# Reciprocal roots of a cross-attention block: one GpSimd power operation in place of eight VectorE steps

## The reference, cut to what matters

```
def _layernorm(x):  m = mean(x); v = var(x); return (x - m) / sqrt(v + 1e-5)
def _rmsnorm(t):    return t * rsqrt(mean(t * t, axis=-1) + 1e-6)        # over the 8 features of a head
q = rmsnorm(heads(layernorm(x) @ Wq.T));  k, v = heads(ctx @ Wk.T, ctx @ Wv.T);  k = rmsnorm(k)
x = x + tanh(g_xattn) * softmax(q k^T / sqrt(8)) v
y = layernorm(x)
x = x + tanh(g_ffn) * down(silu(gate(y)) * up(y))                        # down, gate, up: (w - 128) * scale
```

## Time and profile before

| | |
|---|---|
| Three timed runs | 256.37, 257.71, 260.33 us (median 257.71) |
| Profiled execution, first to last instruction (its own time is recorded as this span alone) | 254.6 us |
| PE busy | 217.0 us, 85% |
| DVE busy | 189.1 us, 74% |
| ACT busy | 176.9 us, 69% |
| POOL busy | 107.6 us, 42% |
| Mean granted clock of PE | 0.966 of full speed |
| Chain that ended last: PE, DVE, issue, ACT | 62%, 17%, 8%, 7% |
| One pass of the loop (two tiles) | 25.05 us |

### The profile page before, as it was taken

One profiled execution on the slowest core, in us unless ns is written; L12 is line 12 of the kernel. 1 busy time (PEld: TensorE's weight loads), 2 busy tenths in 40 slices (PEclk: granted clock), 3 DMA queues, 4 the chain that ended last, 5 costly groups with the idle time before them and its releaser, 6 DMA issues.

```text
span 254.6 us, 7326 instructions
## 1 busy us (share of the span) xinstructions
PE 217.0 (85%) x2592; PEld 175.6 (69%) x2592; DVE 189.1 (74%) x583; ACT 176.9 (69%) x338; POOL 107.6 (42%) x145
## 2 busy tenths in 40 slices
PE   1664878949869999999999999999999998983974
PEld 1553746727558888778878887888788776773873
DVE  4587999872878778786878687968796887667163
ACT  3358593746877896879688958895889588455261
POOL 5012303031314382737184728463835473454442
PEclk9999996777999999999999999999999999999799
DMA  6798631405061524141323223322315041000001
GB/s 176 220 351 209 72 58 21 86 5 107 0 106 35 71 23 86 36 108 33 70 47 97 42 61 61 83 56 51 76 50 64 21 82 48 21 24 0 21 21 41
DMA packets 45128, 18.08 MB, mean 71 GB/s; under 512 B 36401, under 2 KB 44849, under 8 KB 45105
## 3 DMA queue, kind: packets, MB, share of 16 engines
q1 hardware_dynamic: 45104, 17.77, 32.9%
HBM read 7.28 MB, written 2.10 MB: 37 GB/s over the span
## 4 chain that ended last, share of the span: by engine, by line
PE 62%; DVE 17%; issue 8%; ACT 7%; DMA 2%; POOL 2%; SPq 1%; DVEq 0%; ACTq 0%
PE bank L1371 16%; PE bank L1286 14%; PE pv_ps L1250 10%; PE bank L1396 9%; PE score_ps L1231 5%; DVE silu L983 2%; PE bank L1319 2%; ACT probs L530 2%; DVE hidden L998 2%; ACT tanh_g L645 2%; DMA w_raw<-L_xattn_Wv_dram 2%; DVE xc_lo L894 1%; PE bank L1277 1%; PE bank L1273 1%; PE bank L1351 1%
## 5 line engine op out<-in xcount | busy, mean ns | idle before, releaser
L530 ACT ACTIVATE probs<-score_ps 128x1024 f32<-128x1024 f32 x64 | 66.0, 1033 | 2.7 <-PE score_ps L1231 2.7
L466 POOL TENSOR_TENSOR qk_unit<-qk_raw,root_y 128x512 f32<-128x512 f32 x16 | 17.4, 1084 | 86.0 <-DVE root_y L788 86.0
L1371 PE MATMUL bank<-x_hi,gu_hi 128*128 128x256 f32 (+1 forms) x192 | 49.8, 296 | 4.0 <-DVE hidden L998 2.0
L1250 PE MATMUL pv_ps<-probs,v_blocks 128*32 128x128 f32 x1024 | 43.0, 287 | 6.3 <-issue 3.8
L1371 PE MATMUL bank<-x_lo,gu_hi 128*128 128x256 f32 (+1 forms) x192 | 47.1, 281 | 0.0
L434 POOL TENSOR_TENSOR h_lo<-hidden,h_hi 128x256 fp32r<-128x256 f32 (+1 forms) x48 | 36.7, 772 | 21.1 <-ACT h_hi L656 20.3
L1371 PEld LDWEIGHTS bank<-x_hi,gu_hi 128*128 128x128 f32 (+1 forms) x192 | 34.3, 179 | 8.8 <-issue 4.6
L1250 PEld LDWEIGHTS pv_ps<-probs,v_blocks 128*32 128x32 f32 x1024 | 25.1, 112 | 15.8 <-issue 6.6
L1286 PE MATMUL bank<-w_hi,xc_hi 128*128 128x256 f32 x96 | 31.7, 330 | 3.8 <-DVE xc_lo L894 3.8
L1371 PEld LDWEIGHTS bank<-x_lo,gu_hi 128*128 128x128 f32 (+1 forms) x192 | 34.5, 180 | 0.0
L645 ACT ACTIVATE tanh_g<-bank,half_gate 128x256 f32<-128x256 f32 (+1 forms) x48 | 22.7, 474 | 14.8 <-PE bank L1371 13.4
(11 more groups left out here) (108 smaller groups left out, 438.0 us busy)
## 6 DMA issues: line engine op xcount, KB each, us to landing
ctx_sb<-ctx_dram SPq DMA_DIRECT2D x16, 128.0 KB, 2.6
out_dram<-x_all SPq DMA_DIRECT2D x16, 128.0 KB, 1.8
x_all<-x_dram SPq DMA_DIRECT2D x1, 1536.0 KB, 11.3
dn_int<-L_ffn_wq_down_dram SPq DMA_DIRECT2D x1, 704.0 KB, 7.6
gu_int<-L_ffn_wq_gate_dram SPq DMA_DIRECT2D x1, 640.0 KB, 4.6
gu_int<-L_ffn_wq_up_dram SPq DMA_DIRECT2D x1, 640.0 KB, 5.6
x_all<-x_dram SPq DMA_DIRECT2D x1, 384.0 KB, 4.5
w_raw<-L_xattn_Wq_dram SPq DMA_DIRECT2D x1, 256.0 KB, 2.7
```

Source lines behind the costliest of these rows:

```text
L530: nc.scalar.activation(probs[:, t % 2, :], score_ps[t % 2][:].rearrange("p h n -> p (h n)"), ACT.Exp, scale=float(HD) ** 0.5 / UNIT ** 2). ...
L1250: last = nc.tensor.matmul(pv_ps[BLOCK * quadrant:BLOCK * (quadrant + 1), region * P:(region + 1) * P], v_blocks[:, e, h * BLOCK:(h + 1) * ...
L1371: last = nc.tensor.matmul(bank[k][0:r, a * TOK:(a + 1) * TOK], w[:, j, a, c, 0:r], xx[:, c, :], start=(n == 1), stop=(n == (4 if wide_weig ...
```

## The change

The bit estimate and `root_chain` go. POOL does `root_y = root_in ** minus_half` as one `tensor_tensor` with the operation `pow` and a tensor filled with -0.5, for each tile, and likewise for the three batches of x. `roots` moves from DVE's list to POOL's, in front of `qk_norm`; DVE, which now waits for `root_ready` where it waited for the last step, goes on in the meantime with what stands between. `x_roots(0)` stands on POOL ahead of the filling of `v_blocks`. `x_offsets(1)` moves on DVE from behind the means of its batch to behind `root_inputs(-1, 0)`, and `x_offsets(2)` to behind `root_inputs(0, 0)`. The buffers of the middle steps go.

```diff
+            nc.gpsimd.memset(minus_half[:], -0.5).then_inc(half_ready, 1)
+            pool.wait_ge(half_ready, 1)
+            def x_roots(i):
+                first, last = BATCHES[i]
+                pool.wait_ge(x_eps_added, i + 1)
+                nc.gpsimd.tensor_tensor(x_root[:, first:last], x_var[:, first:last], minus_half[:, 0:last - first],
+                                        ALU.pow).then_inc(x_root_ready, 1)
+            x_roots(0)
             nc.gpsimd.memset(v_blocks[:], 0.0).then_inc(v_zeroed, 1)
...
+            x_roots(1)
+            def roots(p, e):
+                b = 2 * p + e
+                if not has_roots(p, b):
+                    return
+                if has_tile(p, b + 2):
+                    pool.wait_ge(eps_added, b + 3)
+                    if since(b, -1):
+                        pool.wait_ge(qk_hi_ready, b + 2)
+                        pool.wait_ge(unit_ready, b + 2)
+                if has_tile(p, b - 1):
+                    pool.wait_ge(root_in_ready, b)
+                if since(b, 2):
+                    pool.wait_ge(x1_bias_ready, b - 1)
+                    pool.wait_ge(x1n_ready, b - 1)
+                nc.gpsimd.tensor_tensor(root_y[:], root_in[:], minus_half[:], ALU.pow).then_inc(root_ready, 1)
...
             def iteration(p):                                   # POOL
+                if isinstance(p, int) and p == FIRST + 1:
+                    x_roots(2)
                 add_attention(p, 0)
                 split_chunks(p - 1, 1, (0, 1))
+                roots(p, 0)
                 qk_norm(p, 0)
                 split_chunks(p, 2, (2,))
                 split_qk(p, 0)
                 split_chunks(p, 2, (3, 4, 5))
                 add_attention(p, 1)
+                roots(p, 1)
                 qk_norm(p, 1)
                 split_qk(p, 1)
...
-            def root_chain(buffers, cols, count, before, first=1, last=ROOT_STEPS):
-                ...                                             # seven scalar_tensor_tensor
...
-                nc.vector.tensor_scalar(root_y[:].bitcast(I32), root_in[:].bitcast(I32), -0.5, START_BITS, ALU.mult,
-                                        ALU.add).then_inc(root_steps, 1)
...
                 root_inputs(p, 0)                               # DVE
+                if first:
+                    x_offsets(1)
+                if second:
+                    x_offsets(2)
                 if isinstance(p, int) and p == PAIRS:
                     up(p, 2, 2)
-                    roots(p, 0, 1, 2)
                     gate(p, 2, 3)
-                    roots(p, 0, 3, 3)
                     up(p, 2, 3)
-                    roots(p, 0, 4, 7)
                     x1_offset(p, 0)
                     gate(p, 2, 4)
                     up(p, 2, 4)
-                elif second:
-                    ...                                         # both chains, step by step in turn
+                else:
                     gate(p, 2, 2)
-                    roots(p, 0, 6, 6)
                     up(p, 2, 2)
-                    roots(p, 0, 7, 7)
                     gate(p, 2, 3)
                     x1_offset(p, 0)
                     up(p, 2, 3)
...
                     root_inputs(p, 1)
-                    roots(p, 1, 1, 1 if early else 4)
                 turn2_lo(p)
                 prep_y(p, 0)
...
-                roots(p, 1, 5, 7)
                 x1_offset(p, 1)
```

More of the change, by code:

```diff
@@ L167, in build_program @@
         x1n = sb("x1n", [P, 2, D])
-        x_root = [sb(f"x_root_{part}", [P, B]) for part in ("in", "y", "xy", "v", "p")]
-        root = [sb(f"root_{part}", [P, 2 * H + 1]) for part in ("in", "y", "xy", "v", "p")]
-        root_in, root_y = root[0:2]
+        x_var = sb("x_var", [P, B])
+        x_root = sb("x_root", [P, B])
+        root_in = sb("root_in", [P, 2 * H + 1])
+        root_y = sb("root_y", [P, 2 * H + 1])
+        minus_half = sb("minus_half", [P, 2 * H + 1])
         xc_hi = sb("xc_hi", [P, 2, 2 * KC, P], F32R)
@@ L231, in build_program @@
         x_eps_added = sem("x_eps_added")
-        x_root_steps = sem("x_root_steps")
+        x_root_ready = sem("x_root_ready")
+        half_ready = sem("half_ready")
         x_bias_ready = sem("x_bias_ready")
@@ L599, in normalize @@
                 nc.scalar.activation(xn[:, 1 - e, :], tile_of(b), ACT.Identity, bias=x_bias[:, one],
-                                     scale=x_root[1][:, one]).then_inc(xn_ready, 1)
+                                     scale=x_root[:, one]).then_inc(xn_ready, 1)
             def normalize2(p, e):
@@ L845, in wait_for_root_buffers @@
                     dve.wait_ge(stats2_ready, b)
[L846 to L849, removed]
+                if since(b, -1):
+                    dve.wait_ge(root_ready, b + 2)
             def root_inputs(p, e):
@@ L876, in x1_offset @@
                 if has_tile(p, b - 1):
-                    dve.wait_ge(root_steps, (ROOT_STEPS + 1) * (b + 3))
+                    dve.wait_ge(root_ready, b + 3)
                     nc.vector.scalar_tensor_tensor(out=x1_bias[:], in0=x1_mean_var[:, 0:1], scalar=-1.0, in1=root_y[:, 2 * H:],
                                                    op0=ALU.mult, op1=ALU.mult).then_inc(x1_bias_ready, 1)
-            def roots(p, e, first, last):
-                b = 2 * p + e
-                if has_roots(p, b):
-                    root_chain(root, slice(0, 2 * H + 1), root_steps, (ROOT_STEPS + 1) * (b + 2), first, last)
             def turn_lo(p, e):
@@ L1090, in begin @@
                     x_means(1)
-                    x_roots(1)
-                    x_offsets(1)
                 out_divide(p, 0)
@@ L1122, in iteration @@
                     up(p, 2, 4)
-                elif second:
-                    for n in range(1, ROOT_STEPS + 1):
-                        roots(p, 0, n, n)
-                        x_roots(2, n, n)
-                    x_offsets(2)
-                    gate(p, 2, 2)
-                    gate(p, 2, 3)
-                else:
-                    roots(p, 0, 1, 5)
-                    gate(p, 2, 2)
-                    roots(p, 0, 6, 6)
+                else:
+                    gate(p, 2, 2)
                     up(p, 2, 2)
-                    roots(p, 0, 7, 7)
                     gate(p, 2, 3)
```

31 lines of the change are left out of this document (6 added, 25 removed).

## The result

The changed kernel takes 417.25 us (416.33 to 417.83), the kernel before 258.94 us in the same comparison: 1.622 times as long, 95% interval 1.6105 to 1.6334. The forecast was 251.4 us, with a range up to 272. It was wrong in sign and size. The rival that ended slower (B) had the direction and the waiting banks of PE right, but even its high end, 309 us, was 108 us short.

What follows compares the result with a forecast made beforehand. PE was taken to bound the loop, with DVE's work paying only at about five places; terms summed to −6.3 us on a 254.6 us span, 248.3, plus 3.1 us for timed runs: 251.4 us, range 247.5 to 272.

Steps and rivals of the forecast that it cites:

- The rival that ended slower (B): Slow power delays POOL's and DVE's lists, so PE's banks drain late; 282.7 us at t = 5, 309 at 6.9; chance 0.30.
- I take eleven passes: t = 1.5 us: Price of one POOL power on 128x65, t: 0.30 us fixed plus eleven plain passes of 0.11 us, 1.5 us.
- The high end, sixty passes or 6.9 us: Upper price of the power: a general power as four times the chain, 60 passes of 0.11 us, 6.9 us.
- t up to about 3.1 us: In the loop, the power may last up to about 3.1 us before PE is later than now.
- below t = 3.1 us each microsecond of t costs about 2 us: Whole kernel: below 3.1 us, one us per us of t at the tail, the other at the start and iteration 0.
- The slope, 14 us for each us of t: Rival B's cost from t = 3.1 us: PE's banks drained late some 14 times, each by the excess of t.
- The sum at t = 1.5 us, −6.3 us: Whole kernel: start 0, iteration 0 −1.6, iteration 1 −1.2, loop −0.7, iteration 7 −0.4, tail −1.9, clock −0.5 us.
- the tail: Iteration 8: an earlier root shortens PE's 3.77 us wait for `hidden`; −1.9 us, each us of t counting in full.
- half of the wait for `xc_lo`: Loop: half of PE's 1.4 us of waits goes, POOL's steps for y still holding up the copies; −0.7 us.
- the 1.6 us that were predicted: Iteration 0: PE's 2.27 us wait for `gu_lo` goes and the next `xc_lo` comes 1.6 us earlier.
- The clock term: Behind PE's long waits, shorter waits may leave its clock high; up to 1.7 us at the tail, −0.5 us taken.
- POOL idles 86.0 us there, so up to that point nothing is lost: In front of `qk_norm`, POOL's idle 86.0 us takes in the power without loss; the argument against rival B.

Runs made afterwards that it cites:

- Experiment 2: Changed kernel with the power on only the last 7 of the 65 columns (1.49 us); 247.61 us, ratio 0.953 to the kernel before.
- experiment 5: Kernel before, roots by VectorE's chain, plus an unused 128x65 power at the same places of POOL's list; 387.59 us, ratio 1.497.
- experiment 1: Changed kernel with a plain product on 128x65 in place of POOL's power; 246.64 us, ratio 0.951 to the kernel before.
- experiments 8 and 10: 8: kernel before with x and layernorm roots by POOL's power, heads by VectorE's chain, 251.38 us; 10: the same with `turn_lo` before `qk_double`, 248.69 us.
- experiments 2 to 4 and 9: 2 to 4: changed kernel, power on 7, 17, 30 columns: 247.61, 259.44, 299.93 us; 9: kernel before plus six POOL operations, power 159 ns a column.

## Why the prediction was wrong

**The step that failed is the price, "I take eleven passes: t = 1.5 us".** Measured are 10.78 us, seven times as much. The fixed part was right (0.30 us estimated from plain operations, 0.4 measured); a column of power costs 159 ns, where a column of a plain two-input operation costs 1.68 ns by the earlier trace rows. Taking a plain pass as the measure for an arithmetic step of a power had no row behind it: the plain loop's pace says what moving a column costs and nothing of how long a function on it takes. The high end, sixty passes or 6.9 us, hung on the same measure and was too low too. With it went the range: it reached to t = 4.2 us.

**The turn, "t up to about 3.1 us", was right for the loop, but not "below t = 3.1 us each microsecond of t costs about 2 us".** At 3.06 us the loop passes are 24.4 to 25.0 us, as before, and the kernel takes 1.006 times the time before. By the sum it should still have been 3 us faster there: between 1.49 and 3.06 us each microsecond costs 7.5 us and not 2; the chain that ended last holds one power at 1.49 us and 12 at 3.06.

**The slope, 14 us for each us of t, was too small.** Measured are 20. I took some 14 delays at which PE's banks are drained late, and did not say which. But at 65 columns all 19 powers of `root_y` lie on the chain that ended last: five ahead of `x_lo` of iteration 1, two up to iteration 2, eight in the loop and four in iterations 6 and 7. Between 5.12 and 10.78 us the same stretches grow by 5.5, 1.6, 9.1 and 4.2 us for each us of t. That is about 1 us for each power in every stretch, also at the start and at the end, and in the loop 1.1 us more than its eight powers, while PE's clock falls. At 10.8 us the rival's formula would have given 259 + 14 × 7.7 − 2 = 365 us; 417 were measured. So of the 166 us by which the forecast missed, some 114 are the price with the slope as I had it, and about 52 the slope; the five uncounted powers, 5 × 7.7, are some 39 of these.

**The sum at t = 1.5 us, −6.3 us, was too small.** Experiment 2 has this duration and gains 8.3 us of span, and 11 us by the medians. The starts of `x_lo` mislead in this comparison, since DVE here runs ahead of PE: in iteration 7 of experiment 2 it starts 2.8 us before PE takes up the gate products that use it, in the kernel before 0.8 us. So the terms are read from the first such product on PE in iterations 1, 6, 7 and 8 (76.04, 200.57, 221.82 and 239.79 us before; 72.35, 194.52, 214.93 and 231.40 in experiment 2):

```profile
221.82 0.36 PE L1371 MATMUL bank<-x_hi,gu_hi 128*128 128x256 f32 x1 [0.17 <-DVE x_lo L1028]
```

```profile
214.93 0.39 PE L1348 MATMUL bank<-x_hi,gu_hi 128*128 128x256 f32 x1
```

| stretch | predicted, us | measured, us |
|---|---|---|
| start to iteration 1 | −2.8 | −3.7 |
| iterations 1 to 6, with the loop | −0.7 | −2.4 |
| 6 to 7 | −0.4 | −0.8 |
| 7 to 8, the tail | −1.9 | −1.5 |
| behind it | 0 | +0.1 |
| clock | −0.5 | in the first row |

In the loop I had taken half of the wait for `xc_lo`; all of it went, and with it 0.2 us a pass that no wait had named. The tail paid nearly what was predicted: PE's wait for `hidden` fell from 3.77 us to 2.70.

```profile
225.91 0.66 PE L1328 MATMUL bank<-ident,x1n 128*128 128x128 f32 x4 [2.70 <-DVE hidden L993]
```

In iteration 0 `xc_lo` starts at 40.00 in place of 41.62 us, the 1.6 us that were predicted, and PE's wait of 2.27 us is gone. The clock term was a true one in the wrong place. Behind the tail's wait it gave nothing: PE's clock is 0.65 over the following 4.8 us in both kernels (with the product of experiment 1, where the wait is 1.78 us, it is 1.00). It paid in iteration 0, where the kernel before does the projection behind the long wait at half the clock and experiment 2 at the full one (windows as in the earlier trace rows, before and experiment 2):

```profile
43.00:47.01 4.01, 4.01 (x23) 4.01 (x19) 3.94 (x8) 1.11 (x3) 0.73 (x1) 0.50 0.75 138
```

```profile
40.14:42.37 2.23, 2.23 (x19) 2.23 (x19) 2.19 (x8) 1.69 (x4) 0.33 (x1) 1.00 0.03 8
```

Part of it is lost again up to iteration 1, in a wait of 1.96 us for the next `gu_lo` that was 0.38 us before.

**"POOL idles 86.0 us there, so up to that point nothing is lost"** was right for the loop: 1.5 us per tile cost nothing there (24.3 to 24.5 us a pass, as with 0.32 us). It was the wrong kind of comfort. 86.0 us of idle time over 16 tiles are 5.4 us each, and a power of 10.78 us is twice that, whoever waits for it; experiment 5 shows that this alone costs 129 us.

**The page's rule.** The Trainium skill, "GPSIMD Engine Reference", section "Performance pitfalls for Q7 kernels", has four cycles per element for each link of a dependent fp32 chain, from which I estimated 3.5 to 6.8 us. It pointed the right way, and the trace agrees with the direction only: it has 159 ns a column. At the page's 1.2 GHz these would be, as an estimate, 191 cycles, or 48 such links. The first call's 6 us of the section "Instruction dispatch" did not show: the first power, on one column, took 0.57 us, on the line of 0.4 us and 159 ns a column.

## What to carry to other kernels

An operation that no row of a profile shows has no price, and an estimate from a neighbour operation of another kind is none; when the slack for it is known (here 3.1 us), ask first what price would be needed, and give the unknown even chances on both sides of it, with a range that reaches as far as the slope carries it. For the slope, count every use of the operation that lies in a chain of dependent steps, at the start and at the end of the kernel too. GpSimd's power was worth its move for 1 to 12 columns (experiments 8 and 10), where it takes the place of a chain of small instructions, and was ruinous for 65. And an engine's idle time in front of a step bounds what may be put there, both for those who wait for the step and for all that stands behind it in that engine's list.

## What the runs showed of the hardware that was not expected

- A GpSimd power on float32 takes 159 ns a column and some 0.4 us, the same on 16 or 128 partitions, for a base of 0.7 or real data, and for the exponents -0.5 and 2.0 (experiments 2 to 4 and 9): 0.57 us at 1 column, 1.49 at 7, 3.06 at 17, 5.12 at 30, 10.78 at 65, 20.79 at 128. A product on 128x65 takes 0.32 us, a thirty-fourth.
- With PE standing still for some 13 of 43 us in every pass, its granted clock is 0.77 and 0.76 in two loop passes; it is 1.00 there in the kernel before.
- The same projection of 18 products on PE in iteration 0 takes 4.01 us at a granted clock of 0.50 (1.2 GHz), behind a wait of 2.27 us and 3.7 us of mixed work, and 2.23 us at 1.00 (2.4 GHz), where that wait is gone.
